# First round of the expert layers: where group 2 is loaded and turned, how the biases come on chip, and where the logits stand

## The reference

```
x = x + PReLU(D^-1/2 A D^-1/2 (LN(x) W) + b)          # the graph layer; its result is called x1
z = LN(x1)                                            # no scale, no shift
logits = mean over all nodes of z @ Wr + br           # one row of 8: one routing for all tokens
p = softmax(logits); p = softmax(p * min(1, capacity / (p * N)))
e0, e1 = top 2 of p; w0, w1 = softmax of their two values
h_e = gelu_erf(z @ W1[e] + b1[e])                     # 256 -> 512, for all nodes
y   = w0 (h_e0 @ W2[e0] + b2[e0]) + w1 (h_e1 @ W2[e1] + b2[e1])
out = x1 + LN(y + z) * gamma + beta
```

## Time and profile before

| | |
|---|---|
| median of three runs | 1192.59 us |
| the profiled execution / its span | 1196.42 / 1194.3 us |
| TensorE busy (PE) | 1155.5 us, 97% |
| TensorE weight loads (PEld) | 988.0 us, 83% |
| VectorE busy (DVE) | 900.9 us, 75% |
| ScalarE busy (ACT) | 596.1 us, 50% |
| GpSimd busy (POOL) | 392.6 us, 33% |
| mean granted clock of TensorE | 0.989 of full speed |

### The profile page before, as it was taken

One profiled execution on the slowest core, in us unless ns is written; L12 is line 12 of the kernel. 1 busy time (PEld: TensorE's weight loads), 2 busy tenths in 40 slices (PEclk: granted clock), 3 DMA queues, 4 the chain that ended last, 5 costly groups with the idle time before them and its releaser, 6 DMA issues. The chain is left out here.

```text
span 1194.3 us, 25237 instructions
## 1 busy us (share of the span) xinstructions
PE 1155.5 (97%) x7395; PEld 988.0 (83%) x7396; DVE 900.9 (75%) x2046; ACT 596.1 (50%) x1521; POOL 392.6 (33%) x476
## 2 busy tenths in 40 slices
PE   7999999999999999999999999999987999999997
PEld 5777888888888888888888888888767999999997
DVE  7897777777877777778777777778465778787785
ACT  5774444444444444444444444444274455565561
POOL 4101233333333333333333333333214234233331
PEclk9999999999999999999999999999998999999999
DMA  8000000000000000000000000000121111111100
GB/s 271 16 2 3 22 21 21 21 21 19 21 20 13 21 21 21 21 19 21 16 16 21 21 21 21 21 20 19 46 82 40 49 44 40 44 48 40 42 28 31
DMA packets 24766, 38.88 MB, mean 33 GB/s; under 512 B 4644, under 2 KB 18574, under 8 KB 24734
## 3 DMA queue, kind: packets, MB, share of 16 engines
q0 software_dynamic: 8480, 22.87, 6.4%
q1 hardware_dynamic: 16254, 15.64, 4.1%
HBM read 25.67 MB, written 12.82 MB: 32 GB/s over the span
## 5 line engine op out<-in xcount | busy, mean ns | idle before, releaser
L1594 PE MATMUL bank<-tab,adj 128*128 128x512 f32 x2401 | 600.5, 399 | 2.2 <-POOL adj L597 2.2
L1594 PEld LDWEIGHTS bank<-tab,adj 128*128 128x128 f32 x2401 | 437.0, 188 | 90.5 <-issue 2.5
L1347 ACT CAST adj<-bank 128x392 fp32r<-128x392 f32 x768 | 317.0, 502 | 320.5 <-PE bank L1576 320.5
L989 DVE TENSOR_TENSOR hot_key<-iota_key,turned 128x588 bf16<-128x588 bf16 (+1 forms) x588 | 260.2, 496 | 0.0
L1576 PEld LDWEIGHTS bank<-hot_key,hot_src 128*128 128x128 bf16 x2304 | 193.4, 146 | 50.6 <-issue 49.4
L1576 PE MATMUL bank<-hot_key,hot_src 128*128 128x147 bf16 (+1 forms) x2304 | 227.9, 248 | 0.0
L981 DVE TENSOR_TENSOR hot_src<-iota_src,turned 128x1536 bf16<-128x1536 bf16 x196 | 187.0, 954 | 23.0 <-issue 12.0
L597 POOL TENSOR_TENSOR adj<-adj,ident 128x128 f32 (+1 forms) x49 | 68.9, 1407 | 385.2 <-ACT adj L1347 384.1
L1194 DVE TENSOR_TENSOR gl<-gf,gh 128x384 fp32r<-128x384 f32 (+1 forms) x136 | 119.3, 904 | 33.0 <-ACT gf L1418 32.6
L1416 ACT ACTIVATE gh<-bank,b1e 128x384 fp32r<-128x384 f32 (+1 forms) x136 | 78.3, 575 | 97.6 <-PE bank L1702 96.9
L1713 PE MATMUL bank<-W2h,gh 128*128 128x256 f32 x392 | 113.2, 289 | 0.0
(11 more groups left out here) (214 smaller groups left out, 1244.5 us busy)
## 6 DMA issues: line engine op xcount, KB each, us to landing
xin<-in_x POOLq DMA_DIRECT2D x49, 128.0 KB, 2.3
x_dram<-x POOLq DMA_DIRECT2D x49, 128.0 KB, 2.0
x1f<-x_dram POOLq DMA_DIRECT2D x16, 384.0 KB, 3.6
out<-res SPq DMA_DIRECT2D x48, 128.0 KB
xs<-in_x SPq DMA_DIRECT2D x2, 1536.0 KB, 13.6
xs<-in_x SPq DMA_DIRECT2D x1, 1664.0 KB, 15.6
xs<-in_x SPq DMA_DIRECT2D x1, 1024.0 KB, 8.4
dst_all<-in_dst SPq DMA_DIRECT2D x1, 816.0 KB, 4.2
```

The lines of the kernel that those rows point to most:

```text
L989: v.tensor_tensor(hot_win[s % 2][j], iota_key[:, lo:hi, :].rearrange("p (o n) c -> p o n c", o=1).to_broadcast(shape), turned[:, k, 1, at: ...
L1347: s.copy(adj[k][:, :].rearrange("p (q n) -> p q n", n=P)[:, :, at:at + GN], adj_ps[j][:, 0:KEYS].rearrange("p (n q) -> p q n", q=T)).then_ ...
L1594: last = mm(acc[k][:, :], adj[k][:, q * P:(q + 1) * P], tab[:, q, :], start=(q == 0), stop=(q == T - 1), skip_group_check=True)
```

## The change

1. The logits' matmuls and `stay_warm(WARM[1])` move from behind the branch into the dense side of it, right behind the sum of z.
2. b1 of all experts is loaded once, with the other constants, as rows of 128 (`b1_rows`, 32 partitions). TensorE turns it into `zsum` behind the branch, ahead of turn 0, and VectorE copies the two experts' columns to `b1e`, each from a column read out of `route_ix`, ahead of `split_z` of group 0. The two word-wise DMAs are gone.
3. `load_expert` is cut in two. W1 of both experts is issued first; SyncE waits until expert 1's W1 has landed and then issues b2 and W2 of expert 0; GpSimd issues b2 and W2 of expert 1 behind the load of group 2.
4. `x1b` of group 0 is made by VectorE right behind `split_z` of group 0, and GpSimd then loads group 2's x1.
5. `b2w` is made by VectorE between tiles 2 and 3 of `split_g` of group 0; GpSimd makes `zb` of group 0 behind it. GpSimd prepares group 1 only behind the last `gl` of group 1.
6. ScalarE takes the gelus of the first two tiles of group 0 ahead of `keep_z` of group 1.
7. TensorE's first round stands outside the loop: hidden 0, hidden 1, first tile of output 0, turn 2, the other two tiles, hidden 2, turn 3, output 1. The loop starts at its second round.

The core of the diff:

```diff
-        def load_expert(eng, k):
+        def load_W1(eng, k):
             eng.wait_ge(rt, ROUTE_IX)
             e = eng.value_load(route_ix[0:1, k:k + 1], min_val=0, max_val=NX - 1)
             eng.dma_start(W1e[:, k, :, :], ...).then_inc(w1_in[k], 16)
-            with nc.allow_non_contiguous_dma(reason="512 biases, once"):
-                eng.dma_start(b1e[:, k, :], ...).then_inc(b1_in[k], 16)
+            return e
+        def load_W2(eng, k, e):
+            eng.dma_start(b2e[:, k, :], ...).then_inc(b2_in[k], 16)
             eng.dma_start(W2e[:, k, :, :], ...).then_inc(w2_in[k], 16)
-            eng.dma_start(b2e[:, k, :], ...).then_inc(w2_in[k], 16)
...
+            sp.dma_start(b1_rows[:, :], a["b1"].rearrange("e (k p) -> (e k) p", p=P)).then_inc(weights_in, 16)
...
-            load_expert(sp, 0)
+            e = load_W1(sp, 0)
+            sp.wait_ge(w1_in[1], 16)
+            load_W2(sp, 0, e)
...
-            load_expert(pool, 1)
+            e = load_W1(pool, 1)
             pool.wait_ge(x1_out, T + 2)
-            pool.wait_ge(rt, ROUTE_END)
-            prepare(0, 0, GT, GT)
+            pool.wait_ge(x1b_first, 1)
+            hold(pool, z_made, GT)
+            g.dma_start(x1f[:, 0, :, :], x1_group(2, GT)).then_inc(x1_in[0], 16)
+            load_W2(pool, 1, e)
+            pool.wait_ge(rt, ROUTE_B2)
+            g.tensor_tensor(zb[:, 0, :, :], zf[:, 0, :, :], bc(b2w, GT), ALU.add).then_inc(prep, PREP)
+            hold(pool, gl_made, 2 + 2 * CF)
             prepare(1, 1, GT, GT)
...
+            dve.wait_ge(b1_turned, 1)
+            for k in range(TOP_K):
+                e = dve.value_load(route_ix[0:1, k:k + 1], min_val=0, max_val=NX - 1)
+                v.tensor_copy(b1e[:, k, :], zsum[:, ds(e * KF + P, KF)]).then_inc(b1_ready, 1)
...
             split_z(0, 0, GT * P)
+            dve.wait_ge(x1_in[0], 16)
+            v.tensor_tensor(x1b[:, 0, :, :], x1f[:, 0, :, :], beta_b, ALU.add).then_inc(x1b_first, 1)
             (W1l of both experts)
+            split_g(0, 0, GT * P, range(2))
             split_z(1, 1, GT * P)
-            split_g(0, 0, GT * P)
+            (b2w, behind b2_in of both experts)
+            split_g(0, 0, GT * P, range(2, CF))
             (W2l of both experts)
-            (b2w)
...
-            keep_z(1, 1, GT * P)
-            for k in range(TOP_K):
-                act.wait_ge(b1_in[k], 16)
-            gelus(0, 0, GT * P, range(CF))
+            act.wait_ge(b1_ready, TOP_K)
+            gelus(0, 0, GT * P, range(2))
+            keep_z(1, 1, GT * P)
+            gelus(0, 0, GT * P, range(2, CF))
...
+                logits()                        # in the dense side, behind the sum of z
+                stay_warm(WARM[1])
...
-            stay_warm(WARM[1])
+            nc.tensor.transpose(zsum[:, P:P + NX * KF], b1_rows[:, :], ident[0:NX * KF, 0:NX * KF]).then_inc(b1_turned, 1)
             turn_z(0, 0, GT)
...
             hidden(0, 0, GT * P)
-            with pe.Fori(0, NG // 2 - 1) as i:
+            hidden(1, 1, GT * P)
+            output(0, 0, GT, lambda: turn_z(2, 0, GT))
+            hidden(2, 0, GT * P)
+            turn_z(3, 1, GT)
+            output(1, 1, GT)
+            with pe.Fori(1, NG // 2 - 1) as i:
```

More of the change, by code:

```diff
@@ L131, in gnn_ffn_kernel @@
         br = sb("br", [1, NX])
+        b1_rows = sb("b1_rows", [NX * KF, P])
         below = sb("below", [P, NCUT, ROWS])
@@ L378, in gnn_ffn_kernel @@
         w1_in = [sem(f"w1_in{k}") for k in range(TOP_K)]
-        b1_in = [sem(f"b1_in{k}") for k in range(TOP_K)]
+        b1_turned = sem("b1_turned")
+        b1_ready = sem("b1_ready")
+        b2_in = [sem(f"b2_in{k}") for k in range(TOP_K)]
+        x1b_first = sem("x1b_first")
         w2_in = [sem(f"w2_in{k}") for k in range(TOP_K)]
@@ L402, in gnn_ffn_kernel @@
         N_CONSTS = 10 + NCUT
-        N_WEIGHTS = 16 * 6
+        N_WEIGHTS = 16 * 7
         EPI = 8
@@ L406, in gnn_ffn_kernel @@
         PREP = 2
-        ROUTE_IX, ROUTE_W, ROUTE_WTS, ROUTE_W1, ROUTE_END = 12, 16, 17, 19, 23
+        ROUTE_IX, ROUTE_W, ROUTE_WTS, ROUTE_W1, ROUTE_B2, ROUTE_END = 12, 16, 17, 19, 21, 23
         ROUTE_EXP = (3, 10, 14)
@@ L460, in load_expert @@
             eng.dma_start(W1e[:, k, :, :], a["W1"][ds(e, 1), :, :].rearrange("e (k p) f -> p (e k) f", p=P)).then_inc(w1_in[k], 16)
-            with nc.allow_non_contiguous_dma(reason="512 biases, once"):
-                eng.dma_start(b1e[:, k, :], a["b1"][ds(e, 1), :].rearrange("e (k p) -> p (e k)", p=P)).then_inc(b1_in[k], 16)
+            return e
+        def load_W2(eng, k, e):
+            eng.dma_start(b2e[:, k, :], a["b2"][ds(e, 1), :].to_broadcast([P, D])).then_inc(b2_in[k], 16)
             eng.dma_start(W2e[:, k, :, :], a["W2"][ds(e, 1), :, :].rearrange("e (k p) d -> p (e k) d", p=P)).then_inc(w2_in[k], 16)
-            eng.dma_start(b2e[:, k, :], a["b2"][ds(e, 1), :].to_broadcast([P, D])).then_inc(w2_in[k], 16)
         @block.sync
@@ L1189, in split_z, with split_g @@
                     v.tensor_tensor(zTl[:, k, q, 0:n], zt_ps[q][:, 0:n], zTh[:, k, q, 0:n].bitcast(F32), ALU.subtract).then_inc(zl_kept, 1)
-            def split_g(g, k, n):
-                for c in range(CF):
+            def split_g(g, k, n, tiles=range(CF)):
+                for c in tiles:
                     dve.wait_ge(g_made, g * (2 * CF) + (2 * c + 10))
@@ L1229, in _ @@
             split_z(0, 0, GT * P)
+            dve.wait_ge(x1_in[0], 16)
+            beta_b = beta_bc[:, :].rearrange("p (o d) -> p o d", o=1).to_broadcast([P, GT, D])
+            v.tensor_tensor(x1b[:, 0, :, :], x1f[:, 0, :, :], beta_b, ALU.add).then_inc(x1b_first, 1)
             for k in range(TOP_K):
@@ L1234, in _ @@
             assert rs[0] == ROUTE_W1 and TOP_K == 2
+            split_g(0, 0, GT * P, range(2))
             split_z(1, 1, GT * P)
-            split_g(0, 0, GT * P)
+            for k in range(TOP_K):
+                dve.wait_ge(b2_in[k], 16)
+            rstep(v.tensor_scalar(b2w[:, :], b2e[:, 0, :], wts[:, 0:1], None, ALU.mult))
+            rsettled()
+            rstep(v.scalar_tensor_tensor(out=b2w[:, :], in0=b2e[:, 1, :], scalar=wts[:, 1:2], in1=b2w[:, :],
+                                         op0=ALU.mult, op1=ALU.add))
+            assert rs[0] == ROUTE_B2
+            split_g(0, 0, GT * P, range(2, CF))
             for k in range(TOP_K):
@@ L1240, in _ @@
                                              in1=W2h[:, k, :, :].bitcast(F32), op0=ALU.mult, op1=ALU.subtract))
[L1241 to L1244, removed]
+            dve.wait_ge(x1b_first, 1)
             assert rs[0] == ROUTE_END
@@ L1431, in _ @@
                 s.copy(W1h[:, k, :, :], W1e[:, k, :, :]).then_inc(w_split, 1)
+            act.wait_ge(b1_ready, TOP_K)
+            gelus(0, 0, GT * P, range(2))
             keep_z(1, 1, GT * P)
-            for k in range(TOP_K):
-                act.wait_ge(b1_in[k], 16)
-            gelus(0, 0, GT * P, range(CF))
+            gelus(0, 0, GT * P, range(2, CF))
             act.wait_ge(rt, ROUTE_WTS)
             for k in range(TOP_K):
-                act.wait_ge(w2_in[k], 2 * 16)
+                act.wait_ge(w2_in[k], 16)
                 s.activation(W2h[:, k, :, :], W2e[:, k, :, :], ACT.Copy, scale=wts[:, k:k + 1]).then_inc(w_split, 1)
@@ L1549, in _, with logits @@
             pe.wait_ge(weights_in, N_WEIGHTS)
+            def logits():
+                pe.wait_ge(rt, 1)
+                for q in range(KD):
+                    last = mm(rt_ps[0:1, 0:NX], zmean[:, q:q + 1], Wr[:, q, :], start=(q == 0), stop=(q == KD - 1))
+                last.then_inc(rt_pe, 1)
             def stay_warm(n):
@@ L1671, in _ @@
                 last.then_inc(zsum_ready, 1)
[L1675 to L1678, removed]
+                logits()
             def turn_z(g, k, n):
@@ L1704, in hidden, with output @@
                         last.then_inc(h1_made, 1)
-            def output(g, k, n):
+            def output(g, k, n, between=None):
                 pe.wait_ge(rt, ROUTE_END)
@@ L1709, in output @@
                 for m in range(n):
+                    if m == 1 and between:
+                        between()
                     pe.wait_ge(norm, (g * GT + m) * NORM + 1)
```

## The result

Six runs of the changed kernel have a median of 1187.1 us (1186.25 to 1190.21), six of the kernel before, the three shown above among them, 1194.63 us (1192.56 to 1196.85). The ratio is 0.9942, 95% interval 0.9922 to 0.9962: 4.5 to 9.3 us faster. The profiled execution took 1189.44 us, its span 1187.8. Timed again, six runs beside other kernels, it was 0.9953 (0.9938 to 0.9968).

What follows compares the result with a forecast made beforehand. TensorE was taken as the bound, with two holes (3.1 us issue, 6.0 us for zf). Terms -1.7 -1.2 -6.0 -2.5 +0.5 +1.0 = -9.9; 9.0 taken off the 1192.59 median gave 1183.6, range 1180 to 1190.

Steps and rivals of the forecast that it cites:

- The main step: Ahead of group 2's turn: its load, issued near 874.6, removes TensorE's hole, -6.0 us; steady clock behind it, -2.5.
- The jump: Ahead of group 0's turn: TensorE's branch jump, about 3.5 us, lies under 12 warming matmuls; turn at 869.7 instead of 872.0.
- The rival of the uncovered jump: Head: warming doesn't hide the jump, turn 0 at 872.1, 4.5 us more, 1188.1; chance 0.20.
- two readings of the Trainium skill: TensorE's jump: 64 queue entries would fit 12 loads and 12 matmuls and cover it; without run-ahead the turn gains nothing.
- The biases' step: VectorE ahead of group 0's split: register loads and copies add 1.3 us (0.9 to 1.8); hidden 0 still 1.7 sooner.
- The head's clock: TensorE idle 2.5 us ahead of turn 1: possible clock fall, priced at +1.0 us (0 to 2.9).
- Hidden 0 and 1: Group 0's and 1's hidden layers, 19.5 us before: fewer waits, -1.2 us (bounds 0 and -2.5).
- that rival: b2 comes late to VectorE, which waits for b2e: +2.6 us, 1186.2; chance 0.08.
- What it adds behind: Third output tile and hidden 2: VectorE waits for GpSimd's powers, group 2's first gl 1 us late; +0.5 us (0 to 2).
- the gap returns in part: VectorE, beside GpSimd, holds the third output tile and group 3's load comes late: +5 us, 1188.6; chance 0.06.
- the slower rival: Loop: its body no longer stays fetched, each of six rounds pays the jump's 3.1 us: +18.6, 1202; chance 0.04.
- The rivals at 1186.2, 1188.1 and 1188.6: Late b2 at VectorE (0.08), uncovered jump in the head (0.20), and the gap ahead of group 2 returning in part (0.06).

Runs made afterwards that it cites:

- round_alone: Kernel before with only the rearranged first round; logits and warming behind the jump, biases by word-wise DMA: 0.9935 of the kernel before.
- warm_in_idle: Changed kernel plus 10 warming matmuls in TensorE's idle time between the turns of groups 0 and 1: 0.9922 of the kernel before.
- the round's two profiles: The profiles of round_alone and round_again, one kernel with only the rearranged first round: 0.9935 and 0.9937 of the kernel before.
- the second profile: The changed kernel as it is, run again beside other kernels on one chip: median 1189.59 us, 0.9953 of the kernel before.
- logits_alone: Kernel before with only the logits and the 12 warming matmuls moved into the dense side: 0.9991 of the kernel before.
- all_steps: Changed kernel with power and third end reordered, warming moved into idle time, expert 1's b2 and W2 earlier, bias copies later: 1182.66 us, 0.9891 of before.
- biases_alone: Kernel before with only the biases loaded as rows, turned on chip and copied by VectorE: 1.0018 of the kernel before.
- no_warming_head: Changed kernel without the 12 warming matmuls behind the logits: run once, no ratio; span ended 322.67 us after the last matmuls of the sum of z began.
- round_again: The kernel of round_alone, run again beside the changed kernel: median 1186.92 us, 0.9937 of the kernel before.

## Why the prediction was right, and where not

*The main step held.* The load of group 2 was issued at S+11.1 (forecast 874.6, which is S+10.9), the hole of 6.0 us went whole and its clock loss with it: from the end of hidden 1 to hidden 2 it was 17.9 us and is 9.1, -8.8 against -8.5 forecast. round_alone has the whole gain of the change.

*The jump held, nearly.* Turn 0 came 2.9 us sooner (forecast 2.3), and 3.46 us was the jump's price (forecast 3.5). It was covered by 4.17 us of warming in the first profile and all but 1.10 us by 2.81 in the second, where turn 0 stood at S+5.12. The rival of the uncovered jump (turn 0 at 872.1, S+8.4) is out. Of the two readings of the Trainium skill weighed there, "TensorE: Matmul & The Clock Gate" (specification table) gives the queue room for all 24 loads and matmuls ahead of the jump; the runs agree as far as 24 instructions go, as the jump is taken about as soon with them as without; a larger number no run tests. The rule of the Trainium skill's "Runtime: NRT & Kernel Launch" (Instruction fetch mechanics), that a taken branch out of the fetched window stalls until a fetch is done, agrees with the 3.46 us.

*The biases' step held in size.* Between the end of wts and group 0's split 1.7 us pass (870.30 to 872.00), 0.1 before: 1.6 added, 1.3 forecast. x1b took 0.95 and the load's issue followed.

*The head's clock was priced too low.* -1.7 and +1.0, -0.7 together, were forecast; -0.4 came. Turn 1 stood where it was forecast (S+9.77 against S+9.8), and hidden 0 came 3.6 us behind it instead of 2.3. That is a small miss at the sum, but the reason given for the lower price was wrong: I read from 2.1 idle us that left the clock at 1.00 that 2.5 might too. It was 3.05 us, and turn 1 was at half clock for most or all of it in all eight profiles whose idle time there was 2.9 to 3.05 us (1.34 to 1.54 us for the turn), with 3.6 to 4.4 us from turn 1 to hidden 0 against 2.2 in warm_in_idle. And the row I read it from doesn't repeat: the round's two profiles had 2.12 and 2.11 idle us there, and the turn took 1.18 and 1.54. The length of the idle time alone doesn't decide it.

*Hidden 0 and 1* took 19.6 us, 19.5 before; -1.2 was forecast, and in the second profile (18.5) -1.0 came. But logits_alone, with the round of before, also took 18.7, so the shorter time isn't shown to be the rearrangement's. b2e came late, as that rival said, but by 0.95 us, not 2.6, and in the second profile not at all.

*What it adds behind was the mis-sized term*: +0.5 forecast (0 to 2), 2.5 measured in P3 - H2, 3.0 to the end. I had named the power, the wait behind it and the late gl, and let VectorE's first gl be 1 us late; it was made 4.5 us after its gelu. The wait for the power came as named (1.74 us), and alone it goes with a P3 - H2 of 19.0 to 19.9, which is 0.5 to 2.0 above the 17.9 to 18.5 of the three kernels with the old round. Left out was the third end's wait for a result buffer, which the store frees (1.61 us), and which comes on top. Both reach TensorE because the third end stands ahead of group 2's first gl; with it moved the loss is gone (17.8 and 17.9). The rival "the gap returns in part" named the right engine and the wrong place: VectorE did hold TensorE up, but group 3's load was not late (no idle time stood ahead of turn 3), and the cost was 2.5 us and not 5.

*The number.* Counted from S, hidden 2 was forecast at 41.4 and came at 42.0 and 40.9 in the two profiles, with hidden 0 and 1 longer and the way from there to hidden 2 shorter than forecast: the errors of the parts cancelled, which is luck. The time, 1187.1, lies inside 1180 to 1190 but above the forecast's own 1181 to 1186.5 and 3.5 us above 1183.6. Of these, 1.5 are gain that didn't come (7.5 instead of 9.0), and 2.0 the median that it was taken from: 1192.59 in three runs, 1194.63 in six. The rivals at 1186.2, 1188.1 and 1188.6 lay as near; the traces and not the time tell them from the forecast. In the slower rival, three late rounds (9.3 us) would have made the time the same and not slower, which takes five.

*What stays open.* Why the single profiles of one kernel differ by up to 2.6 us behind S; only the ratios were used across them. Why the clock fell behind 2.1 idle us in one kernel and not in the other. Why the store's wait stands in some profiles of the same order and not in others. How the round's gain divides among its parts. Whether the logits' move is worth anything beside the other steps of all_steps was not tried.

## What to carry to other kernels

Ask of a buffer that is freed late not only when its load can start, but what stood in order behind the freeing work: moving it left the next consumer (VectorE's ends of the tile and the stores) bunched, and two waits of VectorE ahead of work that a full pipeline was waiting for took 2.5 of the 9.1 us back. Putting two gl ahead of the third of those ends, the same amount of work in another order, saved them. A start made sooner in front of an idle stretch can be lost whole when the clock falls in that stretch (2.0 us sooner at turn 1 in logits_alone, 0.1 at hidden 0); matmuls without use, put into the idle time and not in front of it, kept the clock there, though no gain at the end can be told from that alone. And run each part of a compound change alone: one of three carried the gain, one did nothing that can be told, one cost 0.6 to 3.8 us.

## What the runs showed that was not expected

The twelve warming matmuls behind the logits took 4.17 us in the changed kernel and 2.81 in its second profile, 2.81 in logits_alone and 5.34 in warm_in_idle, whose order of work is the same up to there; and turn 1, behind 2.9 to 3.05 idle us, took 1.51 to 1.54 us instead of 0.87 in each of logits_alone, biases_alone, the changed kernel and no_warming_head, and 1.54 behind 2.11 idle us in round_again. VectorE's `pre` of 256 columns took 1.21 us beside GpSimd's x1b and 0.47 without it.
